# Attention stepped by query tile of four heads, in a four-layer transformer and stencil kernel

## The reference

```python
q = (x @ Wq + bq).reshape(B, S, N_HEAD, HEAD_DIM).transpose(0, 2, 1, 3)   # 16 heads of 32
...
scores = jnp.einsum('bhqd,bhkd->bhqk', q / math.sqrt(HEAD_DIM), k)
scores = scores + attention_bias            # (8, 16, 512, 512) fp32, 134 MB
scores = jnp.where(src_mask, -jnp.inf, scores.astype(jnp.float32))
probs = jax.nn.softmax(scores, axis=-1).astype(v.dtype)
ctx = jnp.einsum('bhqk,bhkd->bhqd', probs, v)
ctx = ctx.transpose(0, 2, 1, 3).reshape(B, S, D)
x = x + (ctx @ Wo + bo)
```

## Time and profile before

| | |
|---|---|
| median of 3 runs | 2963.71 us (2961.55 to 2964.98) |
| the profiled execution | 2961.55 us; its span 2959.7 us |
| PE busy | 2570.2 us (87%) |
| DVE busy | 1992.1 us (67%) |
| ACT busy | 1191.4 us (40%) |
| POOL busy | 915.5 us (31%) |
| first pass, eight sequences | from 90.5 us to 1326 us |

### The profile page before, as it was taken

One profiled execution on the slowest core, in us unless ns is written; L12 is line 12 of the kernel. 1 busy time (PEld: TensorE's weight loads), 2 busy tenths in 40 slices (PEclk: granted clock), 3 DMA queues, 4 the chain that ended last, 5 costly groups with the idle time before them and its releaser, 6 DMA issues.

```text
span 2959.7 us, 44540 instructions
## 1 busy us (share of the span) xinstructions
PE 2570.2 (87%) x12923; PEld 1242.8 (42%) x12923; DVE 1992.1 (67%) x3941; ACT 1191.4 (40%) x2229; POOL 915.5 (31%) x896
## 2 busy tenths in 40 slices
PE   2789898989898888874999998998989999999892
PEld 1344444444444444442344443443434434344340
DVE  4675758485757676667767667676677666776768
ACT  2474747474747465653232222322223222232221
POOL 3222222213222222133514324243152341423416
PEclk8899999999999999997999999999999999999995
DMA  4445545454545463635222213222132222322212
GB/s 136 139 156 143 169 130 172 123 176 132 163 134 162 130 175 116 175 105 198 101 89 80 93 63 128 89 80 86 62 120 80 97 80 75 109 91 82 88 57 85
DMA packets 182947, 345.52 MB, mean 117 GB/s; under 512 B 20354, under 2 KB 50690, under 8 KB 182674
## 3 DMA queue, kind: packets, MB, share of 16 engines
q1 hardware_dynamic: 172882, 324.31, 34.5%
q10 hardware_dynamic: 9792, 17.83, 1.6%
HBM read 298.85 MB, written 17.86 MB: 107 GB/s over the span
## 4 chain that ended last, share of the span: by engine, by line
PE 24%; issue 13%; DVE 9%; POOL 7%; ACT 1%; DVEq 0%; DMA 0%; POOLq 0%; SPq 0%; ACTq 0%
PE ffn_bank L1306 8%; PE ffn_bank L1308 7%; PE ffn_bank L1307 7%; POOL prod L1227 3%; DVE g2T_hi L1598 2%; DVE wl_lo L1604 2%; POOL f L1217 1%; POOL x L1245 1%; DVE tmp L1508 1%; POOL prod L1238 1%; ACT g L1427 1%; PE ffn_bank L1299 1%; DVE tmp L1548 1%; PE ffn_bank L1365 1%; DVE g2T_lo L1599 0%
## 5 line engine op out<-in xcount | busy, mean ns | idle before, releaser
L930 DVE CUSTOM_DVE_ANT_0 negs<-bank,bias 128x512 f32<-128x512 f32 x512 | 341.5, 686 | 153.7 <-PE bank L604 129.8
L737 ACT ACTIVATE prob<-negs,nmax 128x512 f32<-128x512 f32 x512 | 366.3, 716 | 134.4 <-DVE nmax L930 128.7
L614 PE MATMUL bank<-ident,prob 128*128 128x128 f32 x2048 | 334.7, 291 | 66.6 <-ACT prob L737 37.2
L614 PEld LDWEIGHTS bank<-ident,prob 128*128 128x128 f32 x2048 | 264.6, 150 | 209.4 <-ACT prob L737 59.0
L1598 DVE CAST g2T_hi<-g 128x512 f16<-128x512 f32 x256 | 173.6, 678 | 253.2 <-ACT g L1427 249.9
L1599 DVE TENSOR_TENSOR g2T_lo<-g,g2T_hi 128x512 f16<-128x512 f32 x256 | 240.9, 941 | 8.8
L1427 ACT ACTIVATE g<-ffn_bank,bi 128x512 f32<-128x512 f32 x128 | 88.0, 687 | 384.5 <-PE ffn_bank L1308 379.5
L603 PE MATMUL bank<-mask_add,ident_bf 128*128 128x512 bf16 x512 | 206.0, 402 | 40.4 <-DVE nmax L930 40.4
L1306 PE MATMUL ffn_bank<-w_hi,g2T_hi 128*128 128x512 f16 x512 | 200.6, 392 | 45.0 <-DVE g2T_lo L1599 44.8
L1306 PE MATMUL ffn_bank<-x3T_hi,w_hi 128*128 128x512 f16 x512 | 200.1, 391 | 26.8 <-DVE tmp L1548 25.0
L604 PE MATMUL bank<-k_st,q_st 96*128 96x512 f16 x512 | 206.1, 403 | 0.0
(11 more groups left out here) (257 smaller groups left out, 5002.7 us busy)
## 6 DMA issues: line engine op xcount, KB each, us to landing
bias<-in_bias SPq DMA_DIRECT2D x256, 512.0 KB, 3.6
raw<-in_W_l SPq DMA_DIRECT2D x128, 512.0 KB, 3.3
grid<-in_grids SPq DMA_DIRECT2D x172, 256.0 KB, 3.0
q_st<-pT SPq DMA_DIRECT2D x96, 128.0 KB, 5.6
k_st<-pT SPq DMA_DIRECT2D x96, 128.0 KB, 3.1
xin<-in_x SPq DMA_DIRECT2D x9, 1024.0 KB, 5.3
x2n<-x_rows SPq DMA_DIRECT2D x9, 1024.0 KB, 7.0
out<-outt ACTq DMA_DIRECT2D x36, 256.0 KB, 2.0
```

The source lines that it names most:

```text
L614: mm = pe.transpose(bank[:, t * P:(t + 1) * P], prob[:, h % 2, t, j * P:(j + 1) * P], ident[:, :])
L737: act.activation(prob[:, h % 2, j, :], negs[:, j % NT, :], ACT.Exp, scale=-1.0, bias=nmax[:, h % 2, j:j + 1], accum_out=rsum[:, j, h:h + 1 ...
L930: dve.tensor_tensor_reduce(negs[:, j % NT, :], bank[:, :], bias[:, half % NB, j % 2, :], -1.0, 3.0e38, ALU.add, ALU.min, nmax[:, h % 2, j: ...
```

## The change

The unit of work is now a query tile u = 4g + j of four heads (a group g), 16 units in a sequence, instead of a slot of one head.

- q and k stay fp32 (`q32` evicted by ACT, `k32` by DVE); no f16 parts, no stacking transfers. A unit's four masks go into banks 0 to 3, then the four heads' scores as fp32 products of 32 rows each, in the four row strips of the array.
- The reduce writes to `tiles` (three units deep), and Exp works there in place. Four reduces of a unit come before DVE's two evictions of the unit before.
- Transposes are made per query tile: unit u - 1, head i, four key blocks into one bank; ACT evicts heads 0 and 2, DVE heads 1 and 3. Three banks in a ring, shared with `expert`, `up` and `R`.
- Value products are made per half (256 query columns), two key blocks a unit, all groups in bank 7.
- Output products of blocks 0 and 1 come at unit 17 and block 2 before `x1T`.
- L0 parts have new places; bias tiles are loaded as two heads of one query tile.

```diff
-LAG_T = 5
-LAG_PV = 3
-RING_H = 5
-SLOTS_ALL = HT + 11
...
+NQ = G * T
+SLOTS_ALL = NQ + 4
+NR = 3
+def pv_parts(u):
+    return [(v, kb) for v in range(NQ // 2) for kb in range(T) if 2 * v + 3 + kb // 2 == u]
+UP_SLOTS = (2, 3, 4, 6)
+PE_L0 = {4: ("expert",)} | {4 * u: ("up", t) for t, u in enumerate(UP_SLOTS)}
+ACT_L0 = {4: ("expert",)} | {36 + 2 * t: ("scale0", t) for t in range(T)} \
+    | {57 + 2 * t: ("scale1", t) for t in range(T)}
+DVE_L0 = {2: ("g",), 6: ("e",)} | {4 * u + 1: ("y", t) for t, u in enumerate(UP_SLOTS)} \
+    | {26 + 2 * t: ("stats0", t) for t in range(T)} | {50 + 2 * t: ("stats1", t) for t in range(T)}
...
 def attention_slots():
     order, ring = [], 0
+    for u in range(SLOTS_ALL):
+        if u < NQ:
+            order += [(("S", u, i), i) for i in range(4)]
+        for v, kb in pv_parts(u):
+            if v % 2 == 0 and kb == 0:
+                order.append((("ctx", v // 2), 7))
+        keys = extras(PE_L0, u) + [("R", g) for g in range(G) if u == 4 * g + 5]
+        keys += [("T", u - 1, i) for i in range(4)] if 0 < u <= NQ else []
+        for key in keys:
+            order.append((key, 4 + ring % 3))
             ring += 1
     return order
...
+    order = [(("q", c), 4 + c) for c in range(C)]
+    order += [(("k", c), c) for c in range(C)]
+    order += [(("v", t), 4 + t) for t in range(2)]
+    order += [(("xT", c), c) for c in range(C)]
+    order += [(("v", t), 4 + t) for t in range(2, T)] + [(("down",), 4)]
     order += attention_slots()
+    order += [(("x1T", c), 4 + c) for c in range(C)]
+    order += [(("wo", t), t) for t in range(T)]
...
+        q32 = sb("q32", [P, C, S], F32)
+        k32 = sb("k32", [P, C, S], F32)
-        negs = sb("negs", [P, NT, S], F32)
+        tiles = sb("tiles", [P, 4 * NR, S], F32)
-        prob = sb("prob", [P, 2, T, S], F32)
-        pT = sb("pT", [P, RING_H, T, S], F32)
+        pT = sb("pT", [P, 2, 4, T, 2 * P], F32)
...
-                for which, (parts, stack) in enumerate(((qT, q_st), (kT, k_st))):
-                    sp.wait_ge(qk_split, it * 2 * C + (which + 1) * C)
-                    for i in range(4):
-                        for slot in SLOTS:
-                            sp.dma_start(
-                                stack[32 * slot[0]:32 * slot[0] + 32, :, :].rearrange("p (c i) s -> p i c s", i=4)[:, i],
-                                parts[slot[1 + which]][32 * i:32 * i + 32, :, :]).then_inc(qk_stacked, 16)
...
+                def scores(u):
+                    g, j = u // T, u % T
+                    for i in range(4):
+                        bank = claim(pe, it, ("S", u, i))
                         pe.matmul(bank[:, :], ident_bf[:, :], mask_add[:, j, :], start=True, stop=False)
+                    for i in range(4):
+                        rows = slice(HD * i, HD * i + HD)
+                        pe.matmul(psum[i][:, :], q32[rows, g, j * P:(j + 1) * P], k32[rows, g, :],
+                                  start=False, stop=True).then_inc(full[i], 1)
+                def values(v, kb):
+                    g = v // 2
+                    if kb == 0:
+                        if v % 2 == 0:
+                            claim(pe, it, ("ctx", g))
+                        pe.wait_ge(v32_ready, 1 + it * T + T)
+                        for half in range(2):
+                            pe.wait_ge(pT_ready[half], 1 + it * (HT // 2) + 4 * v + 4)
+                    cols = slice((v % 2) * 2 * P, (v % 2) * 2 * P + 2 * P)
+                    for i in range(4):
+                        h = 4 * g + i
+                        mm = pe.matmul(psum[7][HD * i:HD * i + HD, cols], v32[:, kb, h * HD:(h + 1) * HD],
+                                       pT[:, v % 2, i, kb, :], start=kb == 0, stop=kb == T - 1)
+                    if kb == T - 1:
+                        mm.then_inc(pv_done, 1)
...
+                def turn(u, i):
+                    pe.wait_ge(prob_ready, 1 + it * HT + 4 * u + i + 1)
+                    bank = claim(pe, it, ("T", u, i))
+                    for t in range(T):
+                        mm = pe.transpose(bank[:, t * P:(t + 1) * P], tiles[:, 4 * (u % NR) + i, t * P:(t + 1) * P],
+                                          ident[:, :])
+                    mm.then_inc(full_of(("T", u, i)), 1)
+                def out_products(c):
+                    pe.wait_ge(ctx_split, 1 + it * G + c + 1)
+                    for t in range(T):
+                        if c == 0:
+                            claim(pe, it, ("wo", t))
+                        mm = three(psum[t][:, :], [x[:, c, t * P:(t + 1) * P] for x in xT],
+                                   [p[:, c, :] for p in wo], c == 0, c == C - 1)
+                        if c == C - 1:
+                            mm.then_inc(full_of(("wo", t)), 1)
+                for u in range(SLOTS_ALL):
+                    if u < NQ:
+                        scores(u)
+                    for key in extras(PE_L0, u):
+                        l0_products(it, key)
+                    if u == NQ + 1:
+                        out_products(0)
+                        out_products(1)
                     for g in range(G):
+                        if u == 4 * g + 5:
                             bank = claim(pe, it, ("R", g))
                             pe.wait_ge(rinv_ready, it * G + g + 1)
                             for t in range(T):
                                 mm = pe.transpose(bank[:, t * P:(t + 1) * P], rinv_x[:, t, :], ident[:, :])
                             mm.then_inc(full_of(("R", g)), 1)
+                    for v, kb in pv_parts(u):
+                        values(v, kb)
+                    if 0 < u <= NQ:
+                        for i in range(4):
+                            turn(u - 1, i)
+                out_products(2)
                 for c in range(C):
                     l0_products(it, ("x1T", c))
+                out_products(3)
...
+                    bank = arrived(act, it, ("q", m))
+                    act.activation(q32[:, m, :], bank[:, :], ACT.Identity, scale=1.0 / (WS * math.sqrt(HD)),
+                                   bias=bq[:, m:m + 1]).then_inc(q32_ready, 1)
...
+                def evacuate(u, i):
+                    bank = arrived(act, it, ("T", u, i))
+                    act.wait_ge(pv_done, 1 + it * (NQ // 2) + max(0, u // 2 - 1))
+                    act.activation(pT[:, (u // 2) % 2, i, :, (u % 2) * P:(u % 2 + 1) * P],
+                                   bank[:, :].rearrange("p (t q) -> p t q", t=T), ACT.Copy).then_inc(pT_ready[0], 1)
+                for u in range(SLOTS_ALL):
+                    for i in range(4):
+                        n = 4 * u + i
+                        if u < NQ:
+                            tile = tiles[:, 4 * (u % NR) + i, :]
+                            h, j = 4 * (u // T) + i, u % T
+                            act.wait_ge(scored, 1 + it * HT + n + 1)
+                            act.activation(tile, tile, ACT.Exp, scale=-1.0, bias=nmax[:, u % 2, i:i + 1],
+                                           accum_out=rsum[:, j, h:h + 1]).then_inc(prob_ready, 1)
+                        if i % 2 == 0 and 0 < u <= NQ:
+                            evacuate(u - 1, i)
+                        if n in ACT_L0:
+                            l0_part(it, ACT_L0[n])
+                        for g in range(G):
+                            if u == 4 * g + 7 and i == 0:
+                                act.wait_ge(ctx_ready, 1 + it * G + g + 1)
+                                act.activation(xT[0][:, g, :], ctx32[:, :], ACT.Identity, bias=bv[:, g:g + 1])\
+                                    .then_inc(ctx_hi, 1)
+                            if u == 4 * g + 5 and i == 1:
+                                bank = arrived(act, it, ("R", g))
+                                act.wait_ge(ctx_ready, 1 + it * G + g)
+                                act.wait_ge(e_split, it + 2)
+                                act.activation(rinv_T[:, :], bank[:, :], ACT.Copy).then_inc(rinv_T_ready, 1)
...
+                    bank = arrived(dve, it, ("k", m))
+                    dve.tensor_scalar(k32[:, m, :], bank[:, :], 1.0 / WS, bk[:, m:m + 1], ALU.mult, ALU.add)\
+                        .then_inc(k32_ready, 1)
...
+                for u in range(SLOTS_ALL):
+                    for i in range(4):
+                        n = 4 * u + i
+                        if u < NQ:
+                            half = n // 2
+                            bank = arrived(dve, it, ("S", u, i))
+                            if i % 2 == 0:
+                                dve.wait_ge(bias_in[half % NB], (it * (2 * H // NB) + half // NB + 1) * 16)
+                            dve.sem_inc(carrier, 1)
+                            dve.tensor_tensor_reduce(tiles[:, 4 * (u % NR) + i, :], bank[:, :], bias[:, half % NB, i % 2, :],
+                                                     -1.0, 3.0e38, ALU.add, ALU.min, nmax[:, u % 2, i:i + 1])\
```

(41 more changed lines are left out.)

145 lines of the change are left out of this document (14 added, 131 removed).

## The result

The changed kernel takes 2992.03 us, median of 4 runs (2989.13 to 2995.54); the kernel before took 2963.16 beside it (2961.55 to 2964.98). The ratio is 1.0097, 95% interval 1.0085 to 1.011: about 29 us slower. The forecast was 2998.

A forecast was written before the change was run, and what follows sets the result against it. The slot stage was taken as bound by PE work plus waits between three in-order engines. Per sequence 35.4 + 117.4 + 6 = 158.8 us against 154.4, +4.4, times 8 = +35 us: about 2998 us, range 2930 to 3075.

The forecast's parts named there:

- Projections hidden (0 us): Projections of a sequence: the removed f16 splits and stacking transfers were hidden, so 0 us change; 35.4 us kept.
- PE's unit, 4.77: PE's work in one unit: masks, scores, values, switches and transposes, plus 0.1 for a bank wait, 4.77 us.
- the scores' 0.85: Score products of a unit: fp32 in four disjoint row strips, taken as 0.85 us, without switches.
- The unit table: Units 0 to 14: times from one score start to the next, with waits from the engines' orders, sum 87.5 us.
- ACT stands at `scale1`: Unit 14: ACT waits 5.2 us at scale1 for POOL's shift, leaving PE idle 5.1 us in unit 15.
- ACT not held: Rival, tail: POOL's shift comes in time, tail 5.7 us shorter, 153.1 a sequence, 2953 us; chance 0.05.
- The tail, 28.9: End of a sequence, from unit 15's scores through the output products and x1T: 28.9 us at full clock.
- The clock, 6: Slow clock over a sequence: two to three spells, 12 us at half clock, costing 6 us; ends 1 and 12.
- the low edge with 1 for the clock: Low end of the forecast's own span, with slow clock costing 1 us a sequence: 2965 us.
- PE at its own pace: Rival, units 0 to 14: the 10 us of waits a sequence vanish, 80 us in all, 2918 us; chance 0.17.
- Strips serial: Rival, scores: row strips don't run together, 3.4 us in place of 0.85, +248, about 3245 us; chance 0.04.
- clock low for most of the slots: Rival, attention: slow clock costs 12 us a sequence, +48, 3046 us, up to 3080 with slow strips; chance 0.12.

The follow-up runs named there:

- scale1_late: The changed kernel with ACT's four scale1 at slots 61, 64, 65, 67 instead of 57, 59, 61, 63: 2940.21 us, ratio 0.9918 against the kernel before.
- old_kernel_scale1_next: The kernel before with scale1 at slots 52, 54, 56, 58 instead of 56, 58, 60, 62: 3005.7 us, ratio 1.0141.
- spread_tables: The changed kernel with scale1 later, R evicted first, and new places for g, e, stats0 and stats1: 2876.63 us, ratio 0.971 against the kernel before.
- bf16_scores: The changed kernel with q32 and k32 held in bf16 instead of fp32: 2939.2 us, ratio 0.9907 against the kernel before.

## Why the prediction came out right, step by step

The time was forecast as 2998 and is 2992; per sequence +4.4 was forecast and +4.1 measured. The mechanism held, and its larger errors went in opposite directions.

- **Projections hidden (0 us): right.** 35.7 against 35.5, with 7.4 us of DVE's work gone from them.
- **PE's unit, 4.77: 0.1 low.** From start to start in stretches without waits (the row at 358.23 is the second pass asked for by itself; the one above it holds both):

```profile
349.71 2.00 PE L596 MATMUL bank<-ident,tiles 128*128 128x128 f32 x16
351.55 1.03 PE L570 MATMUL bank<-mask_add,ident_bf 128*128 128x512 bf16 x4
352.50 1.14 PE L573 MATMUL bank<-k,q 32*128 32x512 f32 x8
...
357.69 1.14 PE L573 MATMUL bank<-k,q 32*128 32x512 f32 x8
358.23 0.61 PE L573 MATMUL bank<-k,q 32*128 32x512 f32 x4
358.76 1.07 PE L587 MATMUL bank<-pT,v 128*32 128x256 f32 x16
```

  Scores 1.07 (357.69 to 358.76), values 1.00 (358.76 to 359.76), masks 0.95 (351.55 to 352.50), transposes 1.84 (349.71 to 351.55), in all 4.86. The forecast's 4.77 holds 0.1 for a bank wait that these stretches don't have, and its terms for PE's own work add to 4.65 (it says 4.67): the work itself was put 0.2 low. The step that failed is the scores' 0.85, plus one of the switches: 0.97, and it is 1.07. The four strips do run together, as the column strips of the earlier trace rows made likely; the records of the four products start within 0.02 us. But the second pass (358.23) starts 0.53 after the first, not 0.43, and a product's record is 692 ns in the first pass and 587 in the second, against the 0.59 of other fp32 records of 512 columns (lowest, median, highest in ns):

```profile
L573 PE MATMUL bank<-k,q x1024: 587/692/1218, 127.4 to 1329.8; 32*128 32x512 f32 x171
```

  The 3.07 times of the Trainium skill ("TensorE: Matmul & The Clock Gate", Measured speedup vs the span model) gave 1.11 as an estimate for the scores without switches. From the second pass to the values are another 0.54, of which I put 0.11 down to the switch, an estimate (four bf16 strips take 0.33 to the next kind of product, an f16 product in a row of them 0.22). That leaves 0.96 for the scores, 3.5 times less than the 3.4 that I took from the earlier trace rows: between my 0.85 and the page's 1.11, a little nearer to mine.
- **The unit table: right in shape, 2.4 short.** Forecast and measured (first sequence, full clock): u0 5.3 / 5.4, u1 6.2 / 6.1, u2 5.1 / 5.3, u3 5.4 / 5.6, u4 5.4 / 5.6, u5 6.8 / 7.2, u6 5.8 / 6.0, u7 6.3 / 6.3, u8 5.3 / 5.4, u9 8.1 / 8.4, u10 4.8 / 5.0, u11 5.2 / 5.2, u12 5.2 / 5.3, u13 7.4 / 7.7, u14 5.2 / 5.4. Sum 87.5 against 89.9. Of the 0.1 to 0.2 of most units 0.1 is the score block, and units 5, 9 and 13 are 0.3 to 0.4 over. The experiment with `R`'s eviction first took 0.7, 1.4 and 0.7 off them, which shows that ACT's order makes them long.
- **ACT stands at `scale1`: right, and shown by taking it away.** 5.2 forecast, 4.69 measured, with POOL's `shift` as releaser in all seven sequences of the view; PE idle 5.1 forecast, 4.85 measured. `scale1_late` took away 6.5 us a sequence, and `old_kernel_scale1_next` made the same wait in the old kernel. The rival "ACT not held" said 5.7 for the absence of this wait; it is 6.5, with the clock that comes back.
- **The tail, 28.9: 1.6 short.** The mean of seven is 30.5, that of the second sequence 30.3. In it the first output product starts 15.3 us after the last scores (376.11 to 391.44), 14.2 was forecast: values and transposes after the stall ran at half clock, and this was booked under "the clock". From there to q 14.7 was forecast and 15.0 measured, with a gap of about 0.5 us before q (a product of `wo` at 405.73, q at 406.44) that the forecast had not.
- **The clock, 6: too much.** The granted clock over the eight sequences is 0.96, as before: some 12 us a sequence at the lower level, as forecast. What they cost was the error. Of the eight sequences three have units at full clock throughout (89.9 to 90.0); the mean of all is 91.6. That is 1.7, and at most 1.1 more in the tail: 2.8. The spells come where they were forecast, but mostly where ACT or DVE was the bound anyway. This 3.2 too much pays for the 2.4 too little of the units and the 0.5 ahead of q: that the sum came out to 6 us is luck in its terms. Two of its own additions are off besides, to no effect: 2996.7 and 2.2 make 2998.9, and the low edge with 1 for the clock comes to 2958, not 2965.
- **The rival "PE at its own pace" fell.** Its 10 us of waits a sequence between units 0 and 14 are there: all lines of PE's waits on other engines (three of them are shown above), without the 33.9 of the tail's stall, add to 102 us in seven sequences, of which 1.5 a sequence are in the tail: 13 us each. They come from the places in the tables and not from PE's work: with other places, in `spread_tables`, 6.2 of the units' 89.9 us go away.
- **Strips serial, clock low for most of the slots:** both fell; the clock is 0.98 over the units of the second sequence.

What stays open: why spells of slow clock follow the gaps of unit 1 in four sequences and not in the other four, which have the same gaps; and whether the kernel before, with its own tables spread, would not gain as much as the new one did.

## What to carry to other kernels

When work is regrouped, first carry over the distances in the hand-made order: from the last statistics to the scale that needs them, through POOL's 6 us chain. A chain of small instructions on a third engine is invisible in the busy shares, and an in-order engine that comes to wait for its end too early holds everything queued behind it; here one such wait was worth more (52 us) than the whole regrouping lost (29 us). Before pricing a quicker product, find out for each unit which engine's order ends last: 53 of 90 us came, because six units of fifteen were not PE's. And where one version's tables were set in several steps and the other's left alone, as here in the last comparison, the difference need not all be the change's.

## What the runs showed of the hardware that was not expected

- Four fp32 products of 32 rows in four row strips start together and take 1.07 us with the switch to the next kind of product; in bf16 0.33. The fp32 form has two passes, and the second starts 0.53 us after the first; the weight load of a strip takes 184 ns in fp32 against 91 in bf16 (all weight loads of L573, in the new kernel and in `bf16_scores`; lowest, median, highest in ns):

```profile
L573 PEld LDWEIGHTS bank<-k,q x1024: 181/184/333, 127.4 to 1329.4; 32*128 32x128 f32 x171
...
L573 PEld LDWEIGHTS bank<-k,q x512: 90/91/101, 127.0 to 1271.8; 32*128 32x128 bf16 x171
```

- After the stall of 4.85 us the granted clock is 0.51 over 4.5 us, the lower level of 1.2 GHz, though PE is busy in all of them; the sixteen transposes that follow take 3.19 us, 2.08 in `scale1_late` at the same place (its row stands last):

```profile
377.20:382.10 4.90, 0.05 (x5) 0.00 (x1) 2.79 (x9) 2.05 (x5) 2.61 (x9) 0.75 0.09 35
382.10:386.60 4.50, 4.50 (x29) 3.23 (x30) 0.63 (x1) 3.47 (x8) 3.96 (x4) 0.51 1.03 361
...
370.91 2.08 PE L596 MATMUL bank<-ident,tiles 128*128 128x128 f32 x16
```

  All eight stalls of the pass are met or followed by such a spell. In `spread_tables`, where PE's longest wait on a bank in the units is 1.2 us, two spells are left in the first seven sequences.
